# Four normalisations and the last expert of an attention and mixture kernel: work moved from GpSimd to VectorE, and a planner's times changed

## What is computed

```python
def layer(x, ctx, mask):
    n = layernorm(x)                                     # first norm
    q, k, v = n @ Wq.T, ctx @ Wk.T, ctx @ Wv.T           # 16 heads of 16
    s = q @ k / 4, masked by mask and causally
    o = softmax(s) @ v
    x = x + (sigmoid(n @ Wg.T + bg) * o) @ Wo.T
    n = layernorm(x)                                     # second norm
    p = softmax(n @ gate_w)                              # 8 experts
    scale = p where among the two largest, else 0
    for e in range(8):
        a, b = (scale[e] * n) @ w1[e], (scale[e] * n) @ w3[e]
        x = x + (silu(a) * b) @ w2[e]
    return x
```

## Time and profile before

| | us |
|---|---|
| median of 3 runs | 688.75 (688.59 to 693.32) |
| profiled execution, its own time | 690.36 |
| its span in the trace | 688.6 |
| TensorE busy | 653.8 |
| VectorE busy | 469.9 |
| ScalarE busy | 385.0 |
| GpSimd busy | 242.9 |
| mean granted TensorE clock | 0.963 of full speed |

### The profile page before, as it was taken

One profiled execution on the slowest core, in us unless ns is written; L12 is line 12 of the kernel. 1 busy time (PEld: TensorE's weight loads), 2 busy tenths in 40 slices (PEclk: granted clock), 3 DMA queues, 4 the chain that ended last, 5 costly groups with the idle time before them and its releaser, 6 DMA issues.

```text
span 688.6 us, 13557 instructions
## 1 busy us (share of the span) xinstructions
PE 653.8 (95%) x5320; PEld 377.0 (55%) x5320; DVE 469.9 (68%) x969; ACT 385.0 (56%) x778; POOL 242.9 (35%) x293
## 2 busy tenths in 40 slices
PE   7897999999989999999999999999999996899996
PEld 3354455455545445444554445545456675688884
DVE  5684778999866999989987975454423354645452
ACT  2212676766634777777566877677875640232331
POOL 5004123422140305020211614527164535566563
PEclk9898999999996999999999999999999998899997
DMA  6984766010700000000770101003010011012000
GB/s 169 242 118 84 130 129 79 2 21 33 114 11 1 3 3 2 2 33 32 96 181 1 35 1 31 2 3 108 2 44 21 16 33 62 31 62 90 34 31 30
DMA packets 29305, 36.58 MB, mean 53 GB/s; under 512 B 5833, under 2 KB 16457, under 8 KB 29242
## 3 DMA queue, kind: packets, MB, share of 16 engines
q1 hardware_dynamic: 26248, 34.53, 23.7%
q10 hardware_dynamic: 946, 0.92, 0.4%
q0 software_dynamic: 2048, 0.27, 0.3%
HBM read 25.58 MB, written 8.06 MB: 49 GB/s over the span
## 4 chain that ended last, share of the span: by engine, by line
PE 74%; POOL 9%; DVE 7%; issue 6%; ACT 4%; POOLq 0%; ACTq 0%; DVEq 0%
PE bank L1566 18%; PE bank L1544 14%; PE bank L1511 11%; PE bank L1395 11%; PE bank L1630 3%; POOL h_lo L1022 3%; POOL v_sb L1018 3%; PE bank L1632 2%; PE bank L1631 2%; DVE pmax L1284 2%; POOL xn_sb L994 2%; ACT probs L1150 2%; PE bank L1515 2%; DVE v_sb L1374 2%; PE bank L1470 2%
## 5 line engine op out<-in xcount | busy, mean ns | idle before, releaser
L1284 DVE TENSOR_REDUCE pmax<-bank 128x1 f32<-128x512 f32 (+6 forms) x640 | 327.5, 578 | 69.3 <-PE bank L1515 46.8
L1150 ACT ACTIVATE probs<-bank 128x512 f32<-128x512 f32 (+4 forms) x592 | 287.4, 545 | 138.0 <-PE bank L1544 86.8
L1566 PE MATMUL bank<-probs,vaug 128*32 128x256 f32 (+4 forms) x2048 | 156.1, 396 | 0.5 <-ACT probs L1150 0.5
L1544 PE MATMUL bank<-qaug,kaug 64*128 64x512 f32 (+4 forms) x592 | 149.0, 452 | 7.0 <-DVE pmax L1284 3.2
L1511 PE MATMUL bank<-kaug,qaug 62*128 62x512 f32 (+6 forms) x640 | 139.6, 414 | 3.1 <-DVE pmax L1284 1.6
L1544 PEld LDWEIGHTS bank<-qaug,kaug 64*128 64x128 f32 (+1 forms) x592 | 64.4, 185 | 82.3 <-ACT probs L1150 29.8
L1511 PEld LDWEIGHTS bank<-kaug,qaug 62*128 62x128 f32 x640 | 70.7, 189 | 56.5 <-DVE pmax L1284 21.3
L1032 POOL TENSOR_SCALAR nmax<-rmax 128x16 f32<-128x16 f32 x16 | 5.2, 323 | 235.3 <-DVE rmax L1292 235.3
L1566 PEld LDWEIGHTS bank<-probs,vaug 128*32 128x32 f32 (+1 forms) x2048 | 46.5, 109 | 52.1 <-issue 31.1
L1202 ACT ACTIVATE h_hi<-v_sb 128x512 fp32r<-128x512 f32 x32 | 20.2, 632 | 80.5 <-DVE v_sb L1374 79.4
L1022 POOL TENSOR_TENSOR h_lo<-v_sb,h_hi 128x512 fp32r<-128x512 f32 x32 | 41.2, 1288 | 61.3 <-ACT h_hi L1202 61.3
(11 more groups left out here) (137 smaller groups left out, 790.2 us busy)
## 6 DMA issues: line engine op xcount, KB each, us to landing
qaug<-s_dram SPq DMA_DIRECT2D x32, 256.0 KB, 3.3
qaug<-q_parts SPq DMA_DIRECT2D x18, 256.0 KB, 9.2
q_parts<-stage SPq DMA_DIRECT2D x7, 512.0 KB, 2.9
k_parts<-stage SPq DMA_DIRECT2D x4, 512.0 KB, 5.3
w_sb<-in_w SPq DMA_DIRECT2D x4, 512.0 KB, 11.0
out<-x_sb SPq DMA_DIRECT2D x8, 256.0 KB, 2.2
ctx_sb<-in_ctx_t SPq DMA_DIRECT2D x3, 512.0 KB, 5.7
x_sb<-in_x SPq DMA_DIRECT2D x3, 512.0 KB, 6.9
```

The lines of the kernel that those rows point to most:

```text
L1150: act.activation(probs[0:rows, u % NSLOT, h, off:CH], bank_of(e)[0:rows, off:CH], ACT.Exp, scale=DK ** -0.5).then_inc(act_read, 1)
L1284: dve.tensor_reduce(pmax[:, n % 2, qt, h, slot:slot + 1], bank[:, 0:w], AX_X, ALU.max).then_inc(dve_read, 1)
L1544: last.append(pe.matmul(pair[side][0][0:r, off:CH], keys_at(b, ROWS, hp, P * j, r), qaug[b:b + ROWS, p % 2, hp, off:CH], start=True, stop= ...
L1566: last = pe.matmul(psum[O_BANK][32 * h:32 * h + 32, q0:q1], vaug[0:r, col:col + 32], probs[0:r, u % NSLOT, h, q0:q1], start=(j == 0), stop ...
```

## The change

The second norms of the last two chunks in the order, 3 and 0, are computed on VectorE; those of chunks 1 and 2 stay on GpSimd. The planner's time for a norm on GpSimd goes from 2100 to 4900 ns, those of the three rank steps from 500, 750 and 1200 to 900, 1200 and 1800 ns. For the last expert of the last chunk the two GpSimd instructions (product and low half) are on VectorE, and TensorE's six products are regrouped, so that the four that need only `h_hi` come first. The last chunk's output copy is split: ScalarE copies one bank and VectorE the other, each in two halves of 256 columns, and each half's transposes wait for their own half. The planner itself is not told of the last two edits.

```diff
@@ -146,7 +146,7 @@
 
 
 def on_dve(e):
-    return e[0] == "norm" and e[1] == 0 and POS[e[2]] == 0
+    return e[0] == "norm" and (POS[e[2]] >= 2 if e[1] else POS[e[2]] == 0)
 
 
 def projections(p):
...
@@ -242,10 +242,10 @@
 
 
 ALONE = {"bn": ("dve", 750), "stat": ("dve", 1350), "mred": ("dve", 170),
-         "rank0": ("dve", 500), "rank1": ("dve", 750), "rank": ("dve", 1200), "sigmoid": ("act", 3500),
+         "rank0": ("dve", 900), "rank1": ("dve", 1200), "rank": ("dve", 1800), "sigmoid": ("act", 3500),
          "ocopy": ("act", 480), "rexp": ("act", 200), "xs": ("act", 950), "h": ("act", 640),
          "hl": ("act", 640), "ycopy": ("act", 1050)}
-THEN = {"stat": 1050, "mred": 1100, "mT": 2300, "xs": 2300, "ws": 2700, "h": 1200, "hl": 1200, "gm": 750, "norm": 2100}
+THEN = {"stat": 1050, "mred": 1100, "mT": 2300, "xs": 2300, "ws": 2700, "h": 1200, "hl": 1200, "gm": 750, "norm": 4900}
 
 
 def make_plan():
...
@@ -1012,11 +1014,11 @@
                     pool.tensor_copy(w_hi[:, ex, :, :], w_sb[:, ex, :, :]).then_inc(w_hi_ready, 1)
                     pool.wait_ge(w_hi_ready, ex + 1)
                     pool.tensor_tensor(w_lo[:, ex, :, :], w_sb[:, ex, :, :], w_hi[:, ex, :, :].bitcast(F32), ALU.subtract).then_inc(w_lo_ready, 1)
-                elif kind == "h":
+                elif kind == "h" and e[1:] != last_step:
                     i = feed_at[e[1:]]
                     pool.wait_ge(*taken(("b", *e[1:])))
                     pool.tensor_tensor(v_sb[:, i % 2, :], u_sb[i % 2][:, :], v_sb[:, i % 2, :], ALU.mult).then_inc(uv_ready, 1)
-                elif kind == "hl":
+                elif kind == "hl" and e[1:] != last_step:
                     i = feed_at[e[1:]]
                     pool.wait_ge(h_hi_ready, i + 1)
                     pool.tensor_tensor(h_lo[:, i % 2, :], v_sb[:, i % 2, :], h_hi[:, i % 2, :].bitcast(F32), ALU.subtract).then_inc(h_lo_ready, 1)
...
@@ -1188,8 +1190,12 @@
                     act.wait_ge(y_full, E * (POS[c] + 1))
                     if POS[c]:
                         act.wait_ge(pv_done, len(units))
-                    if POS[c] == 3:
-                        act.wait_ge(*made(("yT", ORDER[POS[c] - 2], 1)))
+                    if POS[c] == NC - 1:
+                        act.wait_ge(*made(("yT", ORDER[1], 1)))
+                        for part in range(2):
+                            q = slice(CH // 2 * part, CH // 2 * (part + 1))
+                            act.activation(y_sb[POS[c]][:, 0, q], psum[Y_BANKS[0]][:, q], ACT.Copy).then_inc(y_last[part], 1)
+                        continue
                     for a in range(KD):
                         act.activation(y_sb[POS[c]][:, a, :], psum[Y_BANKS[a]][:, :], ACT.Copy).then_inc(y_copied, 1)
                 elif kind == "hl":
@@ -1251,12 +1257,17 @@
                     step(last)
                     dve.tensor_scalar(var_e[:, :], stat2[:, :, 1], EPS, None, ALU.add).then_inc(var_ready, 1)
                 elif kind == "norm" and on_dve(e):
-                    c = e[2]
-                    dve.wait_ge(rstd_ready, 1)
+                    _, second, c = e
+                    i = norm_at[(second, c)]
+                    dve.wait_ge(rstd_ready, i + 1)
+                    if i:
+                        dve.wait_ge(*made(xn_user(i - 1)))
                     for t in range(TPC):
                         last = dve.tensor_scalar(xn_sb[:, t, :], x_sb[:, TPC * c + t, :], stat2[:, t, 0:1],
                                                  rstd[:, t:t + 1], ALU.subtract, ALU.mult)
                     last.then_inc(xn_ready, 1)
+                    if i:
+                        continue
                     dve.wait_ge(ld["mask"], 16)
                     dve.wait_ge(aug_src, 1)
                     dve.tensor_scalar(idle_rows[0:1, 0:KEYS], mask_i[0:1, :], 0, MASKED, ALU.is_equal, ALU.mult).then_inc(row_ready, 1)
@@ -1369,10 +1380,25 @@
                                              op0=ALU.mult, op1=ALU.mult).then_inc(dve_read, 1)
                 elif kind == "hl":
                     i = feed_at[e[1:]]
+                    if e[1:] == last_step:
+                        dve.wait_ge(*taken(("b", *last_step)))
+                        dve.tensor_tensor(v_sb[:, i % 2, :], u_sb[i % 2][:, :], v_sb[:, i % 2, :], ALU.mult).then_inc(uv_ready, 1)
                     dve.wait_ge(tanh_done, i + 1)
                     dve.wait_ge(uv_ready, i + 1)
                     dve.scalar_tensor_tensor(out=v_sb[:, i % 2, :], in0=t_sb[i % 2][:, :], scalar=1.0, in1=v_sb[:, i % 2, :],
                                              op0=ALU.add, op1=ALU.mult).then_inc(h_ready, 1)
+                    if e[1:] == last_step:
+                        dve.wait_ge(h_hi_ready, i + 1)
+                        dve.wait_ge(h_lo_ready, i)
+                        dve.tensor_tensor(h_lo[:, i % 2, :], v_sb[:, i % 2, :], h_hi[:, i % 2, :].bitcast(F32), ALU.subtract).then_inc(h_lo_ready, 1)
+                elif kind == "ycopy" and e[1] == ORDER[-1]:
+
+                    dve.wait_ge(y_full, E * NC)
+                    dve.wait_ge(*made(("yT", ORDER[1], 1)))
+                    dve.wait_ge(pv_done, len(units))
+                    for part in range(2):
+                        q = slice(CH // 2 * part, CH // 2 * (part + 1))
+                        dve.tensor_copy(y_sb[POS[e[1]]][:, 1, q], psum[Y_BANKS[1]][:, q]).then_inc(y_last[part], 1)
                 elif kind == "yT":
                     _, c, part = e
                     t0 = TPC * c + 2 * part
@@ -1640,17 +1666,30 @@
                             pe.wait_ge(*taken(was))
                     if ex == 0 and POS[c]:
                         pe.wait_ge(y_copied, KD * POS[c])
-                    pe.wait_ge(h_lo_ready, i + 1)
+                    ends = e[1:] == last_step
+                    if ends:
+                        pe.wait_ge(h_hi_ready, i + 1)
+                    else:
+                        pe.wait_ge(h_lo_ready, i + 1)
                     for a in range(KD):
                         hi, lo = (w[:, ex, 2, P * a:P * (a + 1)] for w in (w_hi, w_lo))
                         dst = psum[Y_BANKS[a]][:, :]
                         pe.matmul(dst, hi, h_hi[:, i % 2, :], start=(ex == 0), stop=False)
                         pe.matmul(dst, lo, h_hi[:, i % 2, :], start=False, stop=False)
-                        last = pe.matmul(dst, hi, h_lo[:, i % 2, :], start=False, stop=(ex == E - 1))
+                        if not ends:
+                            last = pe.matmul(dst, hi, h_lo[:, i % 2, :], start=False, stop=(ex == E - 1))
+                    if ends:
+
+                        pe.wait_ge(h_lo_ready, i + 1)
+                        for a in range(KD):
+                            last = pe.matmul(psum[Y_BANKS[a]][:, :], w_hi[:, ex, 2, P * a:P * (a + 1)], h_lo[:, i % 2, :], start=False, stop=True)
                     last.then_inc(y_full, 1)
                 elif kind == "yT":
                     _, c, part = e
-                    pe.wait_ge(y_copied, KD * (POS[c] + 1))
+                    if POS[c] == NC - 1:
+                        pe.wait_ge(y_last[part], KD)
+                    else:
+                        pe.wait_ge(y_copied, KD * (POS[c] + 1))
                     bank = make(e)
                     for t in range(2):
                         for a in range(KD):
```

2 lines of the change are left out of this document (added).

## The result

| | before | with the change |
|---|---|---|
| median, us | 692.85 (686.76 to 697.28, 16 runs) | 685.94 (683.41 to 689.7, 16 runs) |
| ratio | | 0.9925 (95%: 0.990 to 0.995) |
| profiled execution, us | 690.36 | 687.47 |
| its span, us | 688.6 | 685.7 |

The change makes the kernel 0.75% faster, 5.2 us by the ratio (3.5 to 6.9), where 14.3 were forecast. The time of 685.94 us lies above the forecast's range of 667.5 to 681.5. The 16 runs of the kernel before also show that the median of 688.75 us, from which the gain was taken off, lay low in its spread: the new median is 692.85.

The account below looks back on a forecast made before the run. TensorE, busy 653.8 of 688.6 us, was taken as the bound, with its waits and slowed clock as the loss. Terms 4.4 + 0.9 + 2.2 + 1.6 + 1.6 + 3.6 = 14.3 off 688.75 gave 674.5 us, range 667.5 to 681.5.

Parts of the forecast that it names:

- chunk 1 term: Chunk 1's second norm: more products ahead of its transposes end TensorE's 2.40 us wait; gain 4.4 us (2.4 to 6.8).
- rival (b): Last chunk's norm and ranks: GpSimd holds VectorE's instructions, three terms fall to 0.7 us, total 9.6, 679.2 us; 15%.
- The term for chunk 2: Chunk 2's second norm: 3 us more work ahead of its transposes covers a 0.91 us wait; gain 0.9 us (0.5 to 2.5).
- the prediction's signs of being wrong: Profile after: granted clock no better than 0.963, a wait at `mT`, or VectorE instructions stretched where GpSimd runs beside.
- rival (a): Attention stage gives chunk 1's gain back through VectorE's queue or new low-clock stretches; first term about 1, 677.9 us; 14%.
- The last chunk: Last chunk's norm on VectorE, its later ranks and the clock behind them: terms of 2.2, 1.6 and 1.6 us.
- the rank times': Last chunk's ranks: twelve more products ahead cut the scales' wait to 0.9 us; gain 1.6, plus 1.6 from the clock.
- the norm's term: Last chunk's norm on VectorE: TensorE's wait falls to 3.0 us, gain 2.2 (1.4 to 3.1), low clock left as it was.
- rival (c): Low-clock stretches at 214 us and behind the last norm go with the waits: 4.6 us more, 669.9 us; 18%.
- The tail: Last expert and output copy shared between engines: last addition ends sooner; gain 3.6 us (3.0 to 4.0).
- The moved folds: Fold 11 waits for weight splits 1 to 3, but its transposes moved later too; cover 2 us, cost 0.

Follow-up runs that it names:

- e6: The changed kernel with the planner's times of before for chunk 2's second norm and three rank steps alone; 682.55 us, ratio 0.9875.
- e9: The changed kernel with only the planner's time for chunk 2's second norm back at 2100 ns, rank times new; 682.62 us, ratio 0.985.
- e3: The changed kernel, but GpSimd waits for chunk 2's scales before it splits chunk 1's rows and the first expert's weights; 683.97 us, ratio 0.989.
- e2: The changed kernel with only the planner's rank times taken back to 500, 750 and 1200 ns; 689.61 us, ratio 0.997.
- e5: The kernel before with only the last expert's shared steps and the shared output copy; 688.58 us, ratio 0.9955.
- e1: The changed kernel with all the planner's times, norm and rank, as before; 687.34 us, ratio 0.993.
- e7: The changed kernel with all the planner's times as before except the last chunk's rank steps, which keep the new ones; 682.41 us, ratio 0.988.

## Why the prediction was wrong

**The step that failed** stands behind the chunk 1 term: "The later rank steps move only products that nobody waits for, at nothing; cover gone, a wait like the 2.5 us". In chunk 2 the cover was gone, since the new times put the rank steps behind `xs`: the wait was 3.68 us, and the clock was low behind it (0.57 in 391 to 394 us). The low clock is the smaller part, since the kernel before has a low stretch in D too (0.59 in 371 to 375 us). I had the mechanism in hand, in the earlier trace rows: a rank step of 0.41 us that took 2.54 beside GpSimd's `x_lo`. I used it for the last chunk and as rival (b) and never asked where the planner's new times put chunk 2's rank steps against `xs`. The term for chunk 2 was a gain of 0.9; it came, since the norm's wait is gone, and a net loss of 4.6 to 6.4 us (two profiles of each kernel) came with it. That the new times of chunk 2 bring all of it is shown by e6 and e9. That GpSimd's hold on VectorE brings 2.2 to 3.5 of it is shown by e3; the rest comes with the same order of steps, by a way that stays open. This is rival (b)'s mechanism in a place that neither the sum nor the rivals looked at, and the last of the prediction's signs of being wrong, VectorE instructions stretched where GpSimd runs beside. The Trainium skill, "GPSIMD Engine Reference", Key points, says that the two engines contend when VectorE has two SBUF inputs. The trace agrees: 3.33 against 0.41 us.

**The chunk 1 term** was mis-sized: 4.4 forecast. The wait of 2.40 is gone as forecast, and VectorE's idle 4.38 too (0.62 at 209.7). But B fell by 2.3 in the first pair of profiles, and by less on the whole. Five profiles with the old norm time have 85.7 to 88.7 (mean 87.1), eight with the new one 83.8 to 87.6 (mean 85.8): 1.3 us. What failed in it is the clock: the low clock, 2.0 us of the chosen value, does not go with the wait. The first low stretch is still there with the change, with no wait over 0.2 us ahead of it, and the second comes and goes between two executions of the kernel before, with the wait in both. With the change there was another at 221 to 223 us:

```profile
208.00:210.00 2.00, 2.00 (x14) 0.83 (x7) 1.38 (x4) 0.75 (x2) 0.26 (x1) 0.50 0.00 0
...
221.00:223.00 2.00, 2.00 (x20) 0.81 (x16) 1.23 (x5) 1.09 (x4) 0.00 (x0) 0.50 0.00 0
```

In e2, which has the new norm time too, 206 to 210 us are at full clock, so that stretch comes and goes as well. This is rival (a), given 14%: it put the first term at about 1, by new low stretches among other ways.

**The last chunk** was right in its waits and low in its sum: wait for the norm 2.72 (3.0 forecast), norm 2.31 us on VectorE (1.6 to 2.0, or more with GpSimd beside; GpSimd held one of the four instructions, not each as rival (b) had it), wait for the scales 0.53 (0.9). The sum of its terms, 2.2 + 1.6 + 1.6 = 5.4, stands beside 6.0 in the first pair of profiles and 7.3 between the means (80.1 of the kernel before twice and e5, 72.8 of the changed kernel twice). The norm's share is 3.5 to 5.4 (e1's 75.3 against 78.8 and 80.7), where 2.2 were forecast, the rank times' 3.0 (e7), where 3.2 were. What the norm's term lacked is the clock, which the prediction left where it was: the low clock takes 5.1 and 6.8 us of F in the two profiles before, 1.7 in both with the change. That is part of rival (c). By the rule of the Trainium skill, "VectorE: DVE Perf Modes", section on the TRN2 errata, the prediction gave 0.19 us for one of the norm's instructions and a wait 0.8 us shorter, 2.2. The trace disagrees again: the three instructions that were not held took 0.40 us each, and the wait was 2.72.

**The tail** was right: 3.3 to 3.5 against the two profiles of the kernel before (3.6 forecast), in every run that has it; the last addition 6.56 us behind the read of `b`, 6.57 by the steps of the prediction.

**The moved folds** cost nothing that a wait shows. A share of what e3 left in D may be theirs; that was not tried by itself.

**The base.** I took the gain off a median of three runs, 688.75, which many runs put at 692.7. The profile I read was not typical either: 2.0 us short in the start-up, 3.0 long in B. With the right base, 692.85, the forecast would have been 678.5, inside its range and still 7.4 us too low.

**The sum**, with the means of the profiles: 14.3 forecast, less 3.1 for chunk 1 (1.3 instead of 4.4) and 6.4 for chunk 2 (5.5 lost, 178.6 against 173.1, instead of 0.9 gained), more 1.9 for the last chunks (7.3 instead of 5.4), less 0.2 for the tail: 6.5 us. The start-up was longer by 1.7 in the mean of the same profiles, for no reason that the change gives. The measured ratio with its interval is 5.2 us, 3.5 to 6.9.
